# Bringing the top-one results back tile by tile inside the memory stage, splitting the 32-expert weights there, and letting the second product lag by three units

## The chip, the cores and the metric

The kernel runs on one NeuronCore of a Trainium2 chip. The core has five engines with a queue of instructions each: TensorE (PE in the rows; its weight loads are PEld), VectorE (DVE), ScalarE (ACT), GpSimd (POOL) and SyncE (SP, which here only starts transfers). An engine runs its queue in the order in which it was written and waits on semaphores for the others. The metric is the time of one execution on the device in microseconds (us).

## What is computed

The input is 4 sequences of 1024 tokens with 128 channels, in float32. Two layers follow each other, each with a token mixer and an expert network:

```python
x = x + rwkv6_time_mixing(layernorm(x))       # stage 1
x = x + top1_of_8_experts(layernorm(x))       # stage 2, 128 -> 512 -> 128, relu
x = x + quaternion_memory(layernorm(x))       # stage 3, first part
x = x + top4_of_32_experts(layernorm(x))      # stage 3, second part, 128 -> 64 -> 128, swiglu
```

The memory takes keys and values (`x @ Wk.T + bk`, `x @ Wv.T + bv`) as quaternions, makes the keys unit length, sums value times key along the sequence, multiplies the running sum with the conjugate key, divides by the root of the position, normalizes, and projects with `Wo`. The last network takes softmax scores over 32 experts, keeps the four best of each token (with a capacity for each expert), computes `(silu(x @ W1) * (x @ W3)) @ W2` for them and adds one shared expert for all.

## The kernel before

The 4096 tokens are 32 groups of 128, held in `x_tok` (channels along the free axis); four groups are a tile of 512 tokens, so there are 8 tiles (`TILES`). `build` runs three functions one after the other. Each opens its own block, and between two blocks all engines meet.

**Stage 2, `top1_experts` (L622).** Tokens are sorted by expert into rows of DRAM. The loop `over_rows` runs 39 tiles of 128 rows, and GpSimd writes each result back to the DRAM tensor `results` with an indirect transfer (L1092). At its end stand three more pieces of work. The weights of the 32 experts, three tensors of 128 x 2176 (`d_raw`), are split in a rounded high part (`make_hi`, ScalarE, L1174) and the rest (`make_lo`, L1181, one on VectorE and two on GpSimd), since TensorE multiplies them in rounded float32 as three products. SyncE waits for all result rows and brings them back in four transfers (L788). VectorE adds them to `x_tok` in four pieces (L1028). Then the block ends.

**Stage 3, `memory_and_top4` (L1193).** Its planner `weave` (L1357) writes each engine's queue from small functions that name a step. VectorE first sets constants (L1814 to L1823). `norm(i)` normalizes tile i (statistics L1600, step 4), `ahead(i)` makes keys and values, `main(i)` forms value times key (`c_bound`, L1641 on VectorE, L1967 on GpSimd), sums along the sequence on TensorE (L1472) and multiplies with the key again (`c_read`, L1658, L1973), `tail(i)` normalizes and projects (`c_got` L1672, `c_shift` L1687, `x_tok` L1692). After a prologue with `norm(0)`, `ahead(0)`, `norm(1)` come 8 bodies. In body i stand, step by step of 16, `tail(i-1)`, `main(i)`, `ahead(i+1)`, `norm(i+2)`.

Then come 8 tiles of 17 expert units (one shared, 16 pairs). In unit n TensorE makes h1 into `bank_1` and h3 into `bank_3` (three products each, L1507 to L1509), then the second product of unit n-2 (`second`, L1555 to L1558). ScalarE applies silu (L1920), VectorE multiplies with h3 (L1789) and with the routing weights `w_wide` (`hidden`, L1798), ScalarE rounds the result (`hid_hi`, L1930) and GpSimd takes the rest (`hid_lo`, L2000), which the third part of `second` needs. `silu`, `hidden`, `hid_hi` and `hid_lo` have two buffers each. h3 of unit n may overwrite its bank once `hidden` of n-2 is done. Between the units stand the routing of the next tile (`route`, at units 0 to 16, most of its small VectorE work after units 5 to 8 and 11), the statistics of the tile after (`look`; its `look_shift` L1711 after unit 6) and the end of the tile before (`end`: copy of the sum at unit 3, transposes L1589 at unit 4, the add of `x_tok` L1811 at unit 5). SyncE loads `w_wide` for a tile from DRAM in eight transfers of 512 KB.

## Time and profile before

| | us |
|---|---|
| three timed runs | 896.37, 898.77, 899.38 |
| median | 898.77 |
| the profiled execution | 899.56 |
| span of its trace | 897.7 |
| stage 2 ends with its last `x_tok` add, the next block's first VectorE instruction starts | 403.90, 406.88 |
| the expert units start | 551.0 |

| engine | busy us | share |
|---|---|---|
| TensorE | 765.0 | 85% |
| VectorE | 633.8 | 71% |
| GpSimd | 485.7 | 54% |
| ScalarE | 464.0 | 52% |

The profile gives for each instruction its start, duration and inputs, and for the idle time ahead of it which instruction of another engine ended it. Shares of busy time are averages over stages with different limits, so they are read stage by stage. Durations of matmuls overlap, since they are pipelined: two of one kind that follow each other start 0.23 us apart though each shows 0.40.

### The profile page before, as it was taken

How to read it: one execution, taken by the hardware profiler on the slowest of the kernel's cores; microseconds unless marked ns; L12 is line 12 of the kernel's file. 1: busy time of each engine (PE TensorE's matmuls, PEld its weight loads, DVE VectorE, ACT ScalarE, POOL GpSimd, SP SyncE). 2: the span in 40 equal slices, each digit the busy share in tenths (PEclk: the TensorE clock that was granted, in tenths of full speed). 3: DMA queues.
4: the chain of work that ended last, by engine and by line, in shares of the span. 5: the costliest groups of instructions: out<-in, count | busy, mean ns of one | idle time of the engine just before them, and what ended most of it. 6: DMA issues, size and time to landing. Idle time of an engine off the chain costs nothing.

```text
span 897.7 us, 14530 instructions
## 1 busy us (share of the span) xinstructions
PE 765.0 (85%) x3937; PEld 567.5 (63%) x3938; DVE 633.8 (71%) x1453; ACT 464.0 (52%) x918; POOL 485.7 (54%) x440
## 2 busy tenths in 40 slices
PE   5999999996486499912889998999999999999997
PEld 2444444542386499912778786677768686868685
DVE  3789999986564255574587876768686868786764
ACT  3455555652121377722464645656656565756453
POOL 2677777773046344561355653555555555555554
PEclk9999999997555699965899999899999999999998
DMA  5000000000491122220000003545547281909180
GB/s 178 0 1 1 1 0 0 0 1 0 93 375 47 42 66 68 62 106 1 1 2 1 1 1 81 112 91 112 115 88 142 61 168 36 191 20 195 38 166 12
DMA packets 35663, 60.08 MB, mean 67 GB/s; under 512 B 3488, under 2 KB 15264, under 8 KB 34960
## 3 DMA queue, kind: packets, MB, share of 16 engines
q1 hardware_dynamic: 33328, 54.67, 26.1%
q0 software_dynamic: 2272, 4.67, 1.5%
q8 instruction: 27, 0.44, 0.2%
q14 instruction: 36, 0.29, 0.1%
HBM read 51.04 MB, written 8.28 MB: 66 GB/s over the span
## 4 chain that ended last, share of the span: by engine, by line
PE 26%; issue 12%; POOL 11%; DVE 3%; ACT 2%; POOLq 0%; ACTq 0%; DVEq 0%
POOL d_hid_lo L2000 6%; PE c_m L1507 2%; PE c_m L1509 2%; PE c_m L1508 2%; PE c_o L1558 1%; PE c_r L1558 1%; PE c_k L1507 1%; POOL c_bound L1967 1%; PE c_r L1488 1%; PE c_k L1508 1%; PE c_k L1509 1%; POOL c_read L1973 1%; PE c_o L1556 1%; PE c_o L1555 1%; PE c_v L1509 1%
## 5 line engine op out<-in xcount | busy, mean ns | idle before, releaser
L2000 POOL TENSOR_TENSOR d_hid_lo<-c_bound,d_hid_hi 128x512 fp32r<-128x512 f32 x136 | 176.4, 1297 | 157.5 <-ACT d_hid_hi L1930 155.5
L1930 ACT ACTIVATE d_hid_hi<-c_bound 128x512 fp32r<-128x512 f32 x136 | 85.2, 626 | 45.3 <-DVE c_bound L1798 44.9
L576 POOL TENSOR_TENSOR a_rs<-a_r,a_state 128x512 f32<-128x512 f32 x64 | 75.2, 1186 | 29.9 <-DVE a_state L419 28.0
L419 DVE TENSOR_TENSOR_SCAN a_state<-a_decay,a_state,a_vb 128x512 f32<-128x512 f32 x64 | 81.1, 1269 | 0.0
L1092 POOL DMA_INDIRECT results<-b_y_row,b_result_row x39 | 37.4, 960 | 51.1 <-DVE b_y_row L1008 29.8
L1789 DVE TENSOR_TENSOR c_m<-c_bound,c_m 128x512 f32<-128x512 f32 x64 | 44.2, 691 | 26.8 <-PE c_m L1509 20.9
L1789 DVE TENSOR_TENSOR c_v<-c_bound,c_v 128x512 f32<-128x512 f32 x64 | 44.2, 691 | 24.3 <-PE c_v L1509 19.0
L1507 PE MATMUL c_m<-d_x_hi,d_hi 128*128 128x512 f32 x136 | 56.1, 413 | 1.8 <-DVE c_bound L1798 1.6
L999 DVE TENSOR_TENSOR b_hidden<-b_h,b_b 128x512 f32<-128x512 f32 x39 | 27.0, 691 | 42.9 <-PE b_h L835 42.2
L1509 PE MATMUL c_m<-d_x_hi,d_lo 128*128 128x512 f32 x136 | 54.1, 398 | 0.0
L1508 PE MATMUL c_m<-d_x_lo,d_hi 128*128 128x512 f32 x136 | 54.0, 397 | 0.0
L1920 ACT ACTIVATE c_bound<-c_k 128x512 f32<-128x512 f32 x60 | 35.7, 596 | 34.7 <-PE c_k L1509 34.2
L1920 ACT ACTIVATE c_bound<-c_m 128x512 f32<-128x512 f32 x60 | 35.7, 595 | 34.4 <-PE c_m L1509 34.0
L403 DVE TENSOR_TENSOR a_vb<-a_k,a_vb 128x512 f32<-128x512 f32 x64 | 43.1, 685 | 10.4 <-PE a_vb L307 10.4
L559 POOL TENSOR_TENSOR a_xf<-a_lerp,a_xt 128x512 f32<-128x512 f32 x40 | 43.3, 1092 | 10.3 <-DVE a_lerp L396 10.2
L1086 POOL DMA_INDIRECT rows_in<-b_rows,b_index x32 | 31.0, 970 | 31.6 <-DVE b_index L939 22.8
L835 PE MATMUL b_h<-b_xin_t,b_w_now 128*128 128x128 f32 x312 | 43.5, 284 | 0.8 <-ACT b_xin_t L1061 0.4
L843 PE MATMUL b_y<-b_w,b_hidden_t 128*128 x312 | 42.8, 280 | 0.9 <-ACT b_hidden_t L1072 0.7
L1798 DVE TENSOR_TENSOR c_bound<-c_v,d_w_wide 128x512 f32<-128x512 f32 x56 | 38.7, 691 | 6.6 <-DMA d_w_wide<-pair_weights 4.1
L306 PE MATMUL a_vb<-a_v_hi,a_spread 128*128 128x512 f32 x64 | 41.4, 647 | 1.0 <-issue 0.7
L835 PEld LDWEIGHTS b_h<-b_xin_t,b_w_now 128*128 128x128 f32 x312 | 39.6, 199 | 1.9 <-ACT b_xin_t L1069 0.8
L1798 DVE TENSOR_TENSOR c_bound<-c_m,d_w_wide 128x512 f32<-128x512 f32 x56 | 38.7, 691 | 2.5 <-POOL d_hid_lo L2000 0.7
(306 smaller groups left out, 2178.4 us busy)
## 6 DMA issues: line engine op xcount, KB each, us to landing
d_w_wide<-pair_weights SPq DMA_DIRECT2D x64, 512.0 KB, 11.8
b_w<-in_w SPq DMA_DIRECT2D x2, 2048.0 KB
d_raw<-in_moe SPq DMA_DIRECT2D x3, 1088.0 KB
b_xin<-rows_in SPq DMA_DIRECT2D x39, 64.5 KB
b_rows<-results SPq DMA_DIRECT2D x4, 512.0 KB, 5.0
out<-c_read SPq DMA_DIRECT2D x8, 256.0 KB, 2.5
a_weights<-in_mixing SPq DMA_DIRECT2D x1, 901.0 KB
shape_consts<-in_consts SPq DMA_DIRECT2D x1, 744.0 KB
```

The source lines that it names most:

```text
L419: dve.tensor_tensor_scan(state[:, j, seq_cols(h, 1)], decay[:, h, :], vb[j % 3][:, :], first, ALU.mult, ALU.add).then_inc(scan_ready, 1)
L559: pool.tensor_tensor(xf[:, f, :], lerp[:, (f + h) % 2, :], xt[h][:, 1:TILE + 1], ALU.add).then_inc(xf_ready, 1)
L576: pool.tensor_tensor(rs[:, j, :], rr[:, h, :], state[:, j, seq_cols(h, 0)], ALU.mult).then_inc(rs_ready, 1)
L835: mm = pe.matmul(bank_h[h][:, f * P:(f + 1) * P], w1_now[:, h, f * P:(f + 1) * P], xin_t[:, h, :], start=True, stop=True)
L1507: pe.matmul(out, weights_hi, moving_hi, start=start, stop=False)
L1508: pe.matmul(out, weights_hi, moving_lo, start=False, stop=False)
L1509: return pe.matmul(out, weights_lo, moving_hi, start=False, stop=stop)
L1789: dve.tensor_tensor(bank_3[r][:, :], silu[:, r, :], bank_3[r][:, :], ALU.mult).then_inc(product_ready, 1)
L1798: dve.tensor_tensor(hidden[:, r, :], bank_3[r][:, :], w_wide[:, u - 1, :], ALU.mult).then_inc(hidden_ready, 1)
L1920: act.activation(silu[:, r, :], bank_1[r][:, :], ACT.Silu).then_inc(silu_ready, 1)
L1930: act.activation(hid_hi[:, r, :], hidden[:, r, :], ACT.Copy).then_inc(hi_ready, 1)
L2000: pool.tensor_tensor(hid_lo[:, r, :], hidden[:, r, :], hid_hi[:, r, :].bitcast(F32), ALU.subtract).then_inc(lo_ready, 1)
```

## The change

**The split.** The raw weights no longer have tensors of their own: they are loaded into the first 13 of the 16 slices of `w_wide`, which is idle until the expert units. `split_operands` is gone. ScalarE makes the high parts in twelve pieces of 128 x 544, two in each of bodies 0 to 5 (steps 13 and 15). VectorE makes all the rests in twelve such pieces, two in each of bodies 1 to 6 (steps 11 and 15), and some small casts in body 1.

**The results.** SyncE waits for the result rows at the start of stage 3 and brings back one tile at a time into the last three slices of `w_wide` (`BACK_RING` = 3), a further one when a slice has been used. VectorE adds it in step 3 of `norm`, ahead of the statistics. Tiles 0 and 1 are added in the prologue, tiles 2 to 7 in bodies 0 to 5. `results` and `row_stored` are now made in `build`.

**The units.** `second` lags three units (`LAG`) where it lagged two; `hid_hi` and `hid_lo` have three buffers (`HALVES`), `hidden` still two. The steps of `end` move back by one unit each. The constants of stage 1 are freed after it; the unit matrix is kept as `ident`.

```diff
+LAG = 3
+RAW_PAIRS = -(-3 * UNITS * P // TILE)
+BACK_RING = PAIRS - RAW_PAIRS
+SPLITS = 4
+HALVES = 3
...
@@ top1_experts
-                for n in range(4):
-                    sp.wait_ge(row_stored[n], 16 * len(range(n, ROW_TILES, 4)))
-                by_token = results[0:TOKENS, :].rearrange("(p g) c -> p g c", p=P)
-                for n in range(4):
-                    part = slice(n * GROUPS // 4, (n + 1) * GROUPS // 4)
-                    sp.dma_start(back[:, part, :], by_token[:, part, :]).then_inc(come_back[n], 16)
-
+                sp.wait_ge(moe_loaded, 16 * len(moe_in))
...
-                make_small(dve)
-                make_lo(dve, 0)
-                for n in range(4):
-                    dve.wait_ge(come_back[n], 16)
-                    part = slice(n * GROUPS // 4, (n + 1) * GROUPS // 4)
-                    dve.tensor_tensor(x_tok[:, part, :], x_tok[:, part, :], back[:, part, :], ALU.add)
...
-                make_hi(act)
...
-                make_lo(pool, 1)
-                make_lo(pool, 2)
...
@@ memory_and_top4, SyncE
+                def bring_back(i):
+                    sp.dma_start(returned(moe, i), by_token[:, SUB * i:SUB * i + SUB, :]).then_inc(come_back[i % BACK_RING], 16)
+
                 def norm(i, h, step):
+                    if step == 5 and i + BACK_RING < TILES:
+                        sp.wait_ge(x_back, i + 1)
+                        bring_back(i + BACK_RING)
...
+                for n in range(4):
+                    sp.wait_ge(row_stored[n], 16 * len(range(n, ROW_TILES, 4)))
+                for i in range(BACK_RING):
+                    bring_back(i)
...
@@ TensorE
-                    if u >= 2:
-                        second(i, h, u - 2)
-                    elif not (isinstance(i, int) and i == 0):
-                        second(i - 1, 1 - h, UNITS - 2 + u)
+                    if u >= LAG:
+                        second(i, h, u - LAG)
+                    elif i > 0:
+                        second(i - 1, 1 - h, UNITS - LAG + u)
...
@@ VectorE
+                    if step == 3:
+                        dve.wait_ge(come_back[i % BACK_RING], 16 * (i // BACK_RING + 1))
+                        x = x_tok[:, SUB * i:SUB * i + SUB, :]
+                        dve.tensor_tensor(x, x, returned(moe, i), ALU.add).then_inc(x_back, 1)
...
+                    if step in (11, 15) and 0 < i <= 3 * SPLITS // 2:
+                        make_lo(2 * i - 2 if step == 11 else 2 * i - 1)
+                    if step == 14 and i == 1:
+                        dve.tensor_copy(strict[:, :], dw("strict"))
+                        dve.tensor_copy(ones_b[:, :], dw("ones"))
+                        dve.wait_ge(wg_made, 1)
+                        dve.tensor_tensor(wg_lo[:, :], dw("wg"), wg_hi[:, :].bitcast(F32), ALU.subtract).then_inc(small_made, 1)
...
                 def end(i, h, u):
-                    if u == 5:
+                    if u == 6:
...
@@ ScalarE
+                    if step in (13, 15) and i < 3 * SPLITS // 2:
+                        c = 2 * i if step == 13 else 2 * i + 1
+                        n, cols = split_cols(c)
+                        act.activation(hi[n][:, cols], raw_operand(moe, n)[:, cols], ACT.Copy).then_inc(hi_made, 1)
...
@@ split
-                    need(act, unit_out, n - 1)
-                    act.activation(hid_hi[:, r, :], hidden[:, r, :], ACT.Copy).then_inc(hi_ready, 1)
+                    need(act, unit_out, n + 1 - HALVES)
+                    act.activation(hid_hi[:, n % HALVES, :], hidden[:, r, :], ACT.Copy).then_inc(hi_ready, 1)
```

How the queues differ is shown at three places of VectorE's. The names are tiles: `d_` those of the 32-expert network, `c_` those of the memory.

At the changeover, VectorE's queue of before (the branch to L1594 is where the engines meet):

```order
L1008 TENSOR_TENSOR b_y_row<-b_y,b_b 128x128
L1185 CAST d_strict<-d_small 128x128
L1186 CAST d_ones<-d_small 128x128
L1188 TENSOR_TENSOR d_wg_lo<-d_small,d_wg_hi 128x32
L1181 TENSOR_TENSOR d_lo<-d_raw,d_hi 128x2176
L1028 TENSOR_TENSOR x_tok<-x_tok,b_rows 128x1024 x4
L749 UNCONDITIONAL_BRANCH
L1594 UNCONDITIONAL_BRANCH
```

And of the changed kernel, on to the first statistics:

```order
L999 TENSOR_TENSOR b_y_row<-b_y,b_b 128x128
L745 UNCONDITIONAL_BRANCH
L1587 UNCONDITIONAL_BRANCH
...
L1831 CAST c_bias<-memory_weights 64x1536
L1834 TENSOR_TENSOR c_bias<-memory_weights,c_bias 1x1536
L1593 TENSOR_TENSOR x_tok<-x_tok,d_w_wide 128x512
L1598 BN_STATS c_stats<-x_tok 128x6 x4
```

Eight instructions left the end of stage 2, and one add of 128 x 512 stands ahead of the first statistics.

In a memory body, VectorE's queue of before, from the second reading of the keys to the statistics:

```order
L1658 TENSOR_TENSOR c_read<-c_key,c_v 128x512 x2
L1664 TENSOR_TENSOR c_real<-c_v,c_key 128x256
L1664 TENSOR_TENSOR c_real<-c_memory_n,c_key 128x256
L1692 TENSOR_TENSOR x_tok<-c_o,c_kept 128x512
L1672 SCALAR_TENSOR_TENSOR c_got<-c_real,c_r 128x512
L1641 TENSOR_TENSOR c_bound<-c_key,c_v 128x512 x2
```

And of the changed kernel, some rows further on as well:

```order
L1669 TENSOR_TENSOR c_read<-c_key,c_v 128x512 x2
L1636 TENSOR_TENSOR d_lo<-d_w_wide,d_hi 128x544
L1675 TENSOR_TENSOR c_real<-c_v,c_key 128x256
L1675 TENSOR_TENSOR c_real<-c_memory_n,c_key 128x256
L1703 TENSOR_TENSOR x_tok<-c_o,c_kept 128x512
L1636 TENSOR_TENSOR d_lo<-d_w_wide,d_hi 128x544
L1683 SCALAR_TENSOR_TENSOR c_got<-c_real,c_r 128x512
...
L1617 TENSOR_REDUCE c_norm<-c_square 128x128
L1593 TENSOR_TENSOR x_tok<-x_tok,d_w_wide 128x512
L1698 SCALAR_TENSOR_TENSOR c_shift<-c_moments,c_rstd 128x4
L1598 BN_STATS c_stats<-x_tok 128x6 x4
```

Two pieces of the split stand between `c_read` and `c_got`, and the add of the results ahead of `c_shift`.

Between expert units 5 and 7, VectorE's queue of before:

```order
L1795 SCALAR_TENSOR_TENSOR c_bound<-c_v,d_w_wide 128x512
L1811 TENSOR_TENSOR c_read<-x_tok,c_x 128x512
L1735 TENSOR_REDUCE d_total<-d_exps 128x4
L1737 RECIPROCAL d_inverse<-d_total 128x4
L1789 TENSOR_TENSOR c_m<-c_bound,c_m 128x512
L1798 TENSOR_TENSOR c_bound<-c_m,d_w_wide 128x512
L1740 TENSOR_TENSOR d_scores<-d_exps,d_inverse 128x128
L1744 MAX d_top<-d_scores 128x8 x4
L1711 SCALAR_TENSOR_TENSOR d_shift<-d_moments,d_rstd 128x4
```

And of the changed kernel:

```order
L1806 SCALAR_TENSOR_TENSOR c_bound<-c_v,d_w_wide 128x512
L1746 TENSOR_REDUCE d_total<-d_exps 128x4
L1748 RECIPROCAL d_inverse<-d_total 128x4
L1800 TENSOR_TENSOR c_m<-c_bound,c_m 128x512
L1809 TENSOR_TENSOR c_bound<-c_m,d_w_wide 128x512
L1822 TENSOR_TENSOR c_read<-x_tok,c_x 128x512
L1751 TENSOR_TENSOR d_scores<-d_exps,d_inverse 128x128
L1755 MAX d_top<-d_scores 128x8 x4
L1722 SCALAR_TENSOR_TENSOR d_shift<-d_moments,d_rstd 128x4
```

The add of the output (`c_read<-x_tok,c_x`) moved from ahead of unit 6 to behind it, so that it is now followed by the scores and `d_shift`.

## Rows read from the trace of the kernel before

**Rows 1.** Busy time by stretch: from:to, us, then per engine, clock, DMA.
```profile
461.00:476.00 15.00, 13.70 (x106) 12.00 (x104) 11.74 (x34) 8.51 (x23) 8.84 (x9) 1.00 0.01 2
...
655.00:697.00 42.00, 40.26 (x192) 30.77 (x191) 32.14 (x68) 25.98 (x48) 23.13 (x20) 1.00 0.53 109
```

**Rows 2.** Timeline of the changeover: start, us, engine, line, [idle before <- releaser].
```profile
386.19 0.96 POOL L1092 DMA_INDIRECT results<-b_y_row,b_result_row  x1 [0.94 <-DVE b_y_row L1008]
...
388.57 1.76 SPq L788 DMA_DIRECT2D b_rows<-results  x4
...
392.38 2.41 DVE L1181 TENSOR_TENSOR d_lo<-d_raw,d_hi 128x2176 fp32r<-128x2176 f32 x1
...
394.72 9.18 DVE L1028 TENSOR_TENSOR x_tok<-x_tok,b_rows 128x1024 f32<-128x1024 f32 x4
...
406.88 0.06 DVE L1814 MEMSET c_eps<- 128x4 f32 x1 [2.98 <-PEq L2020]
...
410.63 0.87 DVE L1600 BATCH_NORM_STATS2 c_stats<-x_tok 128x6 f32<-128x128 f32 x4
```

**Rows 3.** Instructions on the tile b_rows: landing time of its four returning transfers.
```profile
DMA to landing us min/median/max: 3.7/5.0/6.2
```

**Rows 4.** Timeline of one memory body, VectorE, GpSimd and ScalarE.
```profile
470.36 1.28 DVE L1658 TENSOR_TENSOR c_read<-c_key,c_v 128x512 f32<-128x512 f32 x2
...
470.41 2.52 POOL L1973 TENSOR_TENSOR c_read<-c_key,c_memory_n 128x512 f32<-128x512 f32 x2 [1.12 <-DVE c_memory_n L1652]
...
471.90 1.30 DVE L1664 TENSOR_TENSOR c_real<-c_memory_n,c_key 128x256 f32<-128x256 f32 x1
...
472.88 2.69 POOL L1967 TENSOR_TENSOR c_bound<-c_key,c_value_n 128x512 f32<-128x512 f32 x2
...
475.68 0.69 DVE L1672 SCALAR_TENSOR_TENSOR c_got<-c_real,c_r 128x512 f32<-128x512 f32 x1 [1.87 <-issue]
...
477.13 0.60 ACT L1848 ACTIVATE c_key<-c_k 128x512 f32<-128x512 f32 x1 [3.59 <-PE c_k L1449]
...
480.27 1.22 DVE L1687 SCALAR_TENSOR_TENSOR c_shift<-c_moments,c_rstd 128x4 f32<-128x4 f32 x1 [0.83 <-POOL c_rstd L1983]
```

**Rows 5.** Timeline of the last memory body, one GpSimd and one VectorE instruction.
```profile
541.33 1.02 POOL L1994 TENSOR_TENSOR d_rstd<-d_var_eps,c_minus_half 128x4 f32<-128x4 f32 x1
...
541.79 0.29 DVE L1740 TENSOR_TENSOR d_scores<-d_exps,d_inverse 128x128 f32<-128x128 f32 x1
```

**Rows 6.** Timeline of the expert units, TensorE at its last waits.
```profile
562.19 0.80 PE L1558 MATMUL c_r<-d_hid_lo,d_hi 128*128 128x512 f32 x1 [0.60 <-POOL d_hid_lo L2000]
...
671.05 0.40 PE L1556 MATMUL c_r<-d_hid_hi,d_lo 128*128 128x512 f32 x1
...
672.04 0.50 PE L1558 MATMUL c_r<-d_hid_lo,d_hi 128*128 128x512 f32 x1 [0.58 <-POOL d_hid_lo L2000]
```

**Rows 7.** Timeline of the expert units, VectorE and GpSimd.
```profile
576.05 1.28 POOL L2000 TENSOR_TENSOR d_hid_lo<-c_bound,d_hid_hi 128x512 fp32r<-128x512 f32 x1 [0.49 <-ACT d_hid_hi L1930]
...
576.25 1.10 DVE L1711 SCALAR_TENSOR_TENSOR d_shift<-d_moments,d_rstd 128x4 f32<-128x4 f32 x1
...
656.17 0.69 DVE L1786 SCALAR_TENSOR_TENSOR c_bound<-c_bound,c_m 128x512 f32<-128x512 f32 x1 [0.38 <-PE c_v L1509]
...
661.37 1.31 POOL L2000 TENSOR_TENSOR d_hid_lo<-c_bound,d_hid_hi 128x512 fp32r<-128x512 f32 x1 [0.97 <-ACT d_hid_hi L1930]
...
669.27 0.69 DVE L1798 TENSOR_TENSOR c_bound<-c_v,d_w_wide 128x512 f32<-128x512 f32 x1
```

**Rows 8.** Busy time by stretch where the granted clock rises.
```profile
434.00:435.00 1.00, 1.00 (x7) 1.00 (x7) 1.00 (x5) 0.86 (x4) 0.00 (x0) 0.50 0.00 0
...
435.00:436.00 1.00, 1.00 (x7) 0.79 (x6) 0.81 (x7) 0.33 (x2) 0.19 (x1) 0.90 0.00 0
```

**Rows 9.** Timeline, TensorE: the same product at either clock.
```profile
420.81 2.07 PE L1449 MATMUL c_v<-memory_weights,c_xt 128*128 128x128 f32 x8
...
436.17 1.16 PE L1449 MATMUL c_v<-memory_weights,c_xt 128*128 128x128 f32 x8
```

More of the change, by code:

```diff
@@ L695, in top1_experts @@
         hidden_t = sb("hidden_t", [P, 2, D_FF])
-        back = rows[:, :, :].rearrange("p g c -> p (g c)")[:, 0:TOKENS].rearrange("p (g c) -> p g c", g=GROUPS)
         bank_x = [bank(f"x{n}") for n in range(2)]
@@ L714, in top1_experts @@
         row_loaded = [sem(f"row_loaded{n}") for n in range(4)]
-        row_stored = [sem(f"row_stored{n}") for n in range(4)]
         row_t_out, row_t_ready, h_out, h_ready = sem("row_t_out"), sem("row_t_ready"), sem("h_out"), sem("h_ready")
@@ L718, in top1_experts @@
         ht_ready, y_out, y_ready = sem("ht_ready"), sem("y_out"), sem("y_ready")
-        come_back = [sem(f"come_back{n}") for n in range(4)]
         CHOICE = 5
@@ L763, in _ @@
                     sp.dma_start(tensor[:, :], source).then_inc(early_loaded, 16)
-                load_moe(sp)
+                for tensor, source in zip((moe["small"][:, :], *(raw_operand(moe, n) for n in range(3))), moe_in):
+                    sp.dma_start(tensor, source).then_inc(moe_loaded, 16)
                 sp.wait_ge(early_loaded, 16 * len(early))
@@ L1248, in memory_and_top4 @@
         early_n = late_value
+        come_back = [sem(f"come_back{n}") for n in range(BACK_RING)]
+        x_back = sem("x_back")
+        hi_made, lo_made, wg_made, small_made = sem("hi_made"), sem("lo_made"), sem("wg_made"), sem("small_made")
         half_set, rounded, bias_ready = sem("half_set"), sem("rounded"), sem("bias_ready")
@@ L1355, in memory_and_top4, with split_cols @@
         BY_TANH = (4, 5)
+        def split_cols(c):
+            n, part = divmod(c, SPLITS)
+            width = UNITS * P // SPLITS
+            return n, slice(part * width, (part + 1) * width)
         def weave(engine, norm, ahead, main, tail, look, route, unit, end):
@@ L1400, in _, with ahead @@
             def _(sp):
+                by_token = results[0:TOKENS, :].rearrange("(p g) c -> p g c", p=P)
+                def bring_back(i):
+                    sp.dma_start(returned(moe, i), by_token[:, SUB * i:SUB * i + SUB, :]).then_inc(come_back[i % BACK_RING], 16)
                 def norm(i, h, step):
+                    if step == 5 and i + BACK_RING < TILES:
+                        sp.wait_ge(x_back, i + 1)
+                        bring_back(i + BACK_RING)
+                def ahead(i, h, step):
                     pass
-                ahead = main = tail = look = unit = norm
+                main = tail = look = unit = ahead
                 def route(i, h, u):
@@ L1422, in end @@
                 def end(i, h, u):
-                    if u == 6:
+                    if u == 7:
                         sp.wait_ge(out_ready, i + 1)
@@ L1998, in unit @@
                     pool.wait_ge(hi_ready, n + 1)
-                    need(pool, unit_out, n - 1)
-                    pool.tensor_tensor(hid_lo[:, r, :], hidden[:, r, :], hid_hi[:, r, :].bitcast(F32), ALU.subtract).then_inc(lo_ready, 1)
+                    need(pool, unit_out, n + 1 - HALVES)
+                    pool.tensor_tensor(hid_lo[:, n % HALVES, :], hidden[:, r, :], hid_hi[:, n % HALVES, :].bitcast(F32),
+                                       ALU.subtract).then_inc(lo_ready, 1)
                 def end(i, h, u):
```

86 lines of the change are left out of this document (41 added, 45 removed).

## The prediction

> **What bounds the kernel now.** I read the page's busy shares first, then the busy time by stretch, then the timeline where engines wait. The kernel has three stages, and the change touches three places with three different limits.
>
> The expert units are close to TensorE's limit: it is busy 40.26 us of 42 [rows 1]. What it still waits for is short and repeats in each tile: the third part of a second product waits for `hid_lo` from GpSimd (0.58 us in the row) [rows 6].
>
> A memory body takes 15.0 to 15.3 us. No engine fills it: TensorE 13.70, VectorE 11.74, GpSimd 8.84 of 15 [rows 1]. It is a ring: VectorE works from `c_got` to `c_read` almost without a break, and TensorE's sums then lead to the next `c_got`. VectorE's spare time in it stands in two rows: 1.87 us ahead of `c_got` and 0.83 us ahead of `c_shift` [rows 4]. Work that fits there is free, other VectorE work lengthens the body.
>
> The changeover is pure loss for TensorE. GpSimd has issued its last result row at 386.19 + 0.96 = 387.15. VectorE's share of the split and the `x_tok` adds end at 394.72 + 9.18 = 403.90, the engines meet, VectorE starts the next block at 406.88 after 2.98 us of idle time, and takes the first statistics at 410.63 [rows 2].
>
> **The changeover, part by part.** All of the work between 387.15 and 403.90 leaves the end of stage 2. If the meeting still costs 2.98 us (the same engines, the same clearing of semaphores), VectorE starts at 387.15 + 2.98 = 390.13. Its constants take what they took, 410.63 - 406.88 = 3.75 us, so it is ready for tile 0 at 393.88. SyncE starts the transfers at about 390.13; it need not wait for result rows, because before it could start at 388.57 what waits for the same semaphores [rows 2]. The nearest price of the fetch is the landing time of the four old transfers, 3.7 to 6.2 us for 512 KB each [rows 3]; the new ones have 256 KB, so I take the low end. They land at 393.8, just hidden under the constants. If they take 6.2, 2.5 us of the gain are lost. The add of tile 0 is half of an old piece; the old one shows a quarter of 9.18 us with GpSimd in the way, so the nearest undisturbed instruction is `x_tok` L1692's kind at 0.69 us for 128 x 512, `c_got` in rows 4. First statistics at about 394.57 instead of 410.63: **-16.1 us**.
>
> **What comes back in the memory stage.** The add of tile 1 stands in the prologue, behind a reduction which the chain to the next `c_xn` passes through: +0.7. That of tile 2 lies in body 0, where TensorE runs at half clock and VectorE waits for it: 0. Those of tiles 3 to 7 stand in bodies 1 to 5, right where VectorE waits 0.83 us for `c_rstd` (0.69 fits in 0.83) [rows 4]: 0, if GpSimd's small `c_rstd` instruction doesn't hold VectorE up. It didn't in one place: `d_scores`, with both inputs in SBUF, took its 0.29 us while `d_rstd` ran from 541.33 to 542.35 [rows 5].
>
> The Trainium skill, page "SBUF — State Buffer", section "Who interferes with whom", says otherwise: a VectorE instruction with two SBUF inputs is fully blocked by a GpSimd instruction that reads SBUF and came first, until that ends. By it each of the five adds would be a wait plus 0.69 us late. Rows 5 don't agree for this small instruction, rows 4 do for large ones.
>
> For the large ones the trace is plain: `c_real` with both inputs in SBUF takes 1.30 us where its own work is about 0.4, since it waits until GpSimd's second `c_read` has ended at 470.41 + 2.52 = 472.93; it then goes first, and GpSimd's next instruction is the one that waits [rows 4]. A piece of the split (128 x 544, both inputs in SBUF) costs a quarter of 2.41 us [rows 2], 0.60. The first piece asks at about 471.56, when `c_read` on VectorE ends, 0.1 us ahead of the border between GpSimd's two instructions (470.41 + 1.26 = 471.67). If it wins that border, it runs to 472.3, GpSimd's second `c_read` ends at 473.5, `c_real` at 473.8, `x_tok` at 474.4, the second piece waits for the next border at 475.0 and ends at 475.6, just ahead of `c_got` at 475.68. Cost 0. If it misses it, everything is one GpSimd instruction later and `c_got` comes at 476.9: +1.2 for each of six bodies. I take the first with a small allowance: +0.5 in all. GpSimd's `c_bound` then ends up to 1.2 us later, which its reader on TensorE has in hand. The casts and `d_wg_lo` in body 1 each ask for the port too; one GpSimd instruction more, +1.0. The pieces on ScalarE (nearest row 0.60 for 128 x 512) are two per body and lie in its 3.59 us wait [rows 4]: 0. Sum of the memory stage: **+2.2 us**, between +0.7 and +12.
>
> **The units.** With three units' lag, `hid_lo` is ready one unit earlier than it is needed. The wait at 672.04 goes: the part before started at 671.05 and parts follow each other every 0.23 us, so 672.04 - 671.05 - 0.23 = 0.76 us, 0.8 with the slow restart [rows 6]. Is another wait late next? TensorE is held by VectorE until `hidden` of unit 9 is done at 669.27 + 0.69 = 669.96, because h3 of unit 11 needs its bank. That wait stays. Behind it TensorE has second(8), the ranks, h1 of unit 12 and then h3 of unit 12, which needs `hidden` of unit 10, done some 1.3 us after that of unit 9. So nothing replaces the removed wait. -0.8 in each of tiles 0 to 6, where a routing makes VectorE late; tile 0 has one more at its start (562.19) [rows 6]: -0.8.
>
> Then the moved `end`. Its transposes leave the front of unit 5, so h3 of unit 5 comes sooner and VectorE's 0.38 us wait there shrinks to about 0.1 [rows 7]: -0.3. But the output's add now stands ahead of the scores, which pushes `d_shift` (two SBUF inputs) from 661.37, where it went just ahead of GpSimd's `hid_lo` starting at 661.37, into that instruction. What that costs shows in tile 0, which has no such add ahead of it: GpSimd from 576.05, `d_shift` from 576.25 for 1.10 us instead of 0.14 [rows 7]. `hidden` of unit 9 comes later by this; less the 0.3 and the slack ahead of unit 6's silu, about +0.5 for each of tiles 1 to 5 (tile 6 has no `look`). So tile 0: -1.6; tiles 1 to 5: -0.8 + 0.5 = -0.3 each, -1.5; tile 6: -1.1. Sum **-4.2 us**, between -9 (no block, -1.2 per tile) and +1 (block, and the wait comes back in another place). At the end of the kernel three second products are left instead of two, but they lie beside the last unit's product, rounding and rest: 0.
>
> **Sum.** 899.56 - 16.1 + 2.2 - 4.2 = 881.5 for the profiled execution. The median of the three runs stands 0.8 lower (898.77), so I forecast 880.7, rounded 881.
>
> **The rivals.**
> - *Units gain in full* (`d_shift` gets through): five times 0.9 more, about 4.5, 876.5. For: its delay depends on 0.2 us. Chance 0.15.
> - *The units gain nothing*: the wait for `hid_lo` turns into one for `hidden`, since `hidden` still has two buffers. 881 + 4.2 = 885. Against: the count above. 0.15.
> - *The memory bodies pay*: each piece misses its border (6 x 1.2) and each of five adds is late by 0.7. 7.2 - 0.5 + 3.5 = 10.2 more, 891. By the section of the Trainium skill named above the adds' 3.5 alone would come, 884.5. 0.14.
> - *The changeover gives less*: the meeting, the fetch or the first add costs 2.5 to 4 us more, 884. 0.10.
> - *Slower than before: the clock.* TensorE's granted clock is 0.50 (1.2 GHz) up to 435 and rises after continuous work from 430 on [rows 8]. A group of eight matmuls takes 2.07 us there against 1.16 at 2.4 GHz [rows 9]. If VectorE's extra waits keep TensorE from rising, a body of 13.70 us busy becomes 13.70 x 1.78 = 24.4, +9.4. It decides from the third such body on: 881 + 28 = 909. Against: the adds and pieces leave TensorE's gaps about as long as they are. 0.03.
> - *The change doesn't do what it says*: the next block's start doesn't move, because something else holds the meeting. Nothing in rows 2 between 387.15 and 403.90 is left that could. 0.01, 897.
>
> My forecast's case has 0.42. The range from 872 to 890 holds it, the first two rivals, the fourth, and half of the third. Faster by over 0.3% (2.7 us, what a measurement of this kernel can tell from no change): 0.95; within: 0.02; slower: 0.03.
>
> **What would show it.** In the changed trace: first `c_stats` 7.5 us after the last indirect store is issued, with no wait for a transfer ahead of the first add. Bodies 1 to 5 of 15.0 to 15.6 us, adds of 0.69 and not 1.3, `c_got` still with an idle time ahead of it. In the units no wait of TensorE for `hid_lo`, periods shorter by some 0.3 to 0.5 us, and `d_shift` at 1.1 instead of 0.14. It is wrong if bodies grow by over 1 us or if TensorE's waits for `hidden` grow by what those for `hid_lo` lose.

## Result and the profile after

The changed kernel takes **885.84 us** (median of 4 runs, 883.27 to 886.19) against 899.08 us of the kernel before beside it: ratio 0.985, 95% interval 0.982 to 0.988. The forecast was 881, between 872 and 890. The profiled execution spans 884.3 us instead of 897.7.

To see where the 13.4 us went I cut both executions at four instructions: the start of the last indirect store, the first statistics of stage 3 (`c_stats`), and the first and the last `hid_lo` on GpSimd.

| stretch | before | after | change | forecast |
|---|---|---|---|---|
| start to last indirect store | 386.19 | 387.36 | +1.2 | 0 |
| to the first statistics | 24.44 | 12.65 | -11.8 | -16.1 |
| to the first `hid_lo` (memory stage) | 144.41 | 146.45 | +2.0 | +2.2 |
| to the last `hid_lo` (units) | 334.78 | 330.21 | -4.6 | -4.2 |
| to the end | 7.9 | 7.6 | -0.3 | 0 |

The first two rows hold the whole miss. The +1.2 is not the change's by all that shows: in the twelve kernels of this document, whose first two stages have nearly the same work up to there, the last store starts anywhere from 381.4 to 387.4 (385.7 to 387.4 in all but two), and the kernel before lies among the others with its 386.19. The -11.8 is the change's.

The changeover after, where [rows 2] showed it before (timeline; start, us, engine, line, and in brackets the idle time before and its releaser):

```profile
387.36 0.96 POOL L1076 DMA_INDIRECT results<-b_y_row,b_result_row  x1 [0.94 <-DVE b_y_row L999]
395.53 0.06 DVE L1825 MEMSET c_eps<- 128x4 f32 x1 [8.96 <-PEq L2041]
...
395.58 4.75 SPq L1375 DMA_DIRECT2D d_w_wide<-results  x4
...
397.50 1.75 DVE L1834 TENSOR_TENSOR c_bias<-memory_weights,c_bias 1x1536 fp32r<-1x1536 f32 x1
399.28 0.69 DVE L1593 TENSOR_TENSOR x_tok<-x_tok,d_w_wide 128x512 f32<-128x512 f32 x1
400.01 0.87 DVE L1598 BATCH_NORM_STATS2 c_stats<-x_tok 128x6 f32<-128x128 f32 x4
```

The constants take 3.75 us as before, the add of tile 0 takes 0.69 and has no wait for a transfer ahead of it: all as forecast. But GpSimd has issued its last store at 388.32, no engine has work, and VectorE starts at 395.53, **7.21 us** later instead of 2.98.

What happens in them stands in another view, the instructions of one source line, here the line that opens stage 2's block (columns: queue, kind, duration in ns min/median/max, start). After:

```profile
L745 DVEq DRAIN  x1: 303/303/303, 386.3 to 386.3; - x1
L745 POOLq DRAIN  x1: 7067/7067/7067, 387.1 to 387.1; - x1
```

and the same line of the kernel before:

```profile
L749 POOLq DRAIN  x1: 15792/15792/15792, 389.5 to 389.5; - x1
...
L749 DVEq DRAIN  x1: 7803/7803/7803, 396.1 to 396.1; - x1
```

At the end of a block each engine executes a DRAIN, which holds until its earlier work is done. VectorE's ends with its last instruction. GpSimd's doesn't. After, it ends at 387.1 + 7.07 = 394.2, 5.9 us behind the last store's instruction. Before, it ended at 389.5 + 15.79 = 405.3, which is again 5.9 us behind GpSimd's last instruction, the piece of the split that ended at 387.64 + 11.78 = 399.42. So before the change the 5.9 us ran beside VectorE's `x_tok` adds (to 403.90), and of the 2.98 us that I read as the price of the meeting, the first 1.4 (403.90 to 405.3) were the end of this drain. After, the 7.21 us are 5.9 of drain and 1.3 from its end to VectorE's start.

A memory body after, where [rows 4] showed one before:

```profile
455.69 1.01 POOL L2000 TENSOR_TENSOR c_rstd<-c_var_eps,c_minus_half 128x4 f32<-128x4 f32 x1
455.82 0.68 DVE L1593 TENSOR_TENSOR x_tok<-x_tok,d_w_wide 128x512 f32<-128x512 f32 x1
...
456.73 1.23 DVE L1698 SCALAR_TENSOR_TENSOR c_shift<-c_moments,c_rstd 128x4 f32<-128x4 f32 x1 [0.23 <-POOL c_rstd L2000]
...
461.80 3.01 POOL L1990 TENSOR_TENSOR c_read<-c_key,c_memory_n 128x512 f32<-128x512 f32 x2 [1.12 <-DVE c_memory_n L1663]
462.96 0.72 DVE L1636 TENSOR_TENSOR d_lo<-d_w_wide,d_hi 128x544 fp32r<-128x544 f32 x1
...
465.62 1.20 DVE L1636 TENSOR_TENSOR d_lo<-d_w_wide,d_hi 128x544 fp32r<-128x544 f32 x1
467.08 0.69 DVE L1683 SCALAR_TENSOR_TENSOR c_got<-c_real,c_r 128x512 f32<-128x512 f32 x1 [0.27 <-issue]
```

The add takes 0.68 us although GpSimd's `c_rstd` was first, and lies in the wait ahead of `c_shift`, which shrank from 0.83 to 0.23. The first piece of the split got between GpSimd's two `c_read` (they take 3.01 together instead of 2.52), and the idle time ahead of `c_got` fell from 1.87 to 0.27: used up, but not overrun.

The units after, where [rows 6] and [rows 7] showed them before (VectorE, GpSimd, TensorE):

```profile
650.24 1.30 POOL L2017 TENSOR_TENSOR d_hid_lo<-c_bound,d_hid_hi 128x512 fp32r<-128x512 f32 x1 [0.46 <-ACT d_hid_hi L1947]
...
650.61 0.96 DVE L1722 SCALAR_TENSOR_TENSOR d_shift<-d_moments,d_rstd 128x4 f32<-128x4 f32 x1
...
656.43 0.50 PE L1496 MATMUL c_m<-d_x_hi,d_hi 128*128 128x512 f32 x1 [1.13 <-DVE c_bound L1809]
...
660.09 0.50 PE L1496 MATMUL c_v<-d_x_hi,d_hi 128*128 128x512 f32 x1 [1.29 <-DVE c_bound L1809]
```

No wait for `hid_lo` is left but one of 0.6 us at the very end of the kernel, and `d_shift` (128 x 4) takes 0.96 us, because it asks 0.4 us after GpSimd's `hid_lo` has started. Counted from the tile's first `hid_lo`, `d_shift` comes at 14.7 us instead of 14.9, not later than before; it is GpSimd's instruction that moved further, from 14.9 to 14.3, since unit 6's products no longer stand behind the output's add.

### The profile page after: what moved, and what is told of

It reads as the page before. It is cut to its first block, busy times and chain, and to the rows that moved or that the text cites. A ratio compares the mean times of both kernels' runs of the same rounds, so it can differ in the third digit from the quotient of the medians.

```text
span 884.3 us, 14563 instructions
## 1 busy us (share of the span) xinstructions
PE 759.0 (86%) x3937; PEld 572.3 (65%) x3938; DVE 639.8 (72%) x1468; ACT 463.6 (52%) x927; POOL 479.7 (54%) x438
## 4 chain that ended last, share of the span: by engine, by line
PE 31%; issue 8%; POOL 7%; DVE 6%; ACT 2%; DMA 1%; POOLq 0%; SPq 0%; DVEq 0%; ACTq 0%
PE c_m L1496 3%; PE c_m L1498 3%; PE c_m L1497 3%; POOL d_hid_lo L2017 2%; PE c_v L1496 1%; PE c_k L1496 1%; PE c_o L1550 1%; PE c_k L1497 1%; PE c_k L1498 1%; POOL c_bound L1984 1%; PE c_o L1547 1%; PE c_o L1548 1%; POOL c_read L1990 1%; PE c_v L1498 1%; PE c_r L1550 1%
## 5 line engine op out<-in xcount | busy, mean ns | idle before, releaser
L1076 POOL DMA_INDIRECT results<-b_y_row,b_result_row x39 | 37.5, 960 | 51.9 <-DVE b_y_row L999 35.3
L834 PEld LDWEIGHTS b_y<-b_w,b_hidden_t 128*128 128x128 f32 x312 | 38.5, 194 | 3.0 <-issue 2.1
```

The costliest lines, as they stand in the source:

```text
L834: mm = pe.matmul(bank_y[h][:, 0:P], hidden_t[:, h, f * P:(f + 1) * P], w2[:, bass.ds(e * D_FF + f * P, P)], start=(f == 0), stop=(f == FF_ ...
```

## Experiments

Every kernel is compared with the kernel before, run beside it on the same chip. "Changed" is the changed kernel. It did not run beside the others, so a difference to it carries about 1 us of doubt (the kernel before has medians of 899.08 to 900.08, and 895.30 in a single run); where a difference is smaller than some 2 us, only the stretches of the traces tell it.

| kernel | us | before beside it | ratio, 95% interval |
|---|---|---|---|
| changed | 885.84 | 899.08 | 0.985 (0.982 to 0.988) |
| c_gp_filler | 890.23 | 900.08 | 0.990 (0.987 to 0.994) |
| c_no_drain | 880.13 | 900.08 | 0.978 (0.975 to 0.982) |
| c_mid_drain | 884.95 | 900.08 | 0.984 (0.980 to 0.988) |
| c_skip_first | 880.50 (one run) | 899.32 | |
| b_skip | 894.01 (one run) | 895.30 | |
| u_lag_two | 890.86 | 900.08 | 0.990 (0.986 to 0.994) |
| u_shift_first | 880.92 | 899.32 | 0.980 (0.977 to 0.984) |
| u_end_early | 878.83 (one run) | 895.30 | |
| m_small_early | 884.77 (one run) | 899.32 | |
| best1 | 875.63 | 899.32 | 0.975 (0.972 to 0.978) |

### Is it the drain? Work put ahead of it, the drain left out

> The changed kernel with one more GpSimd instruction at the end of stage 2, a subtraction of 128 x 2176 behind the last indirect store (some 5.8 us by the 11.78 us that two of them took in rows 2); its result is not used, nothing is left out. In the changed kernel GpSimd's drain at the end of the block starts at 387.1 and ends at 394.2, 5.9 us after the last indirect store's instruction (387.36 + 0.96 = 388.32); in the kernel before it ended at 405.3, 5.9 us after the last piece of the split (387.64 + 11.78 = 399.42). Theory: a drain on GpSimd, after it has issued indirect transfers, costs 5.9 us counted from the end of its last instruction, however long ago the transfers landed. So the meeting moves by the whole filler: kernel 5.5 to 6.0 us slower than the changed one (885.8), about 891.5. Rival, the drain only waits until the last store's data has landed: the filler lies in that wait, 0 to 0.5 us, about 886. Rival, the meeting costs 7 us after the last engine for another reason (code of the next block): also 5.5 to 6 slower, but then the runs without the drain show no gain.

```diff
                 over_rows(pool, tile)
+                more = rows[:, 0:17, 0:P]
+                pool.tensor_tensor(more, more, more, ALU.subtract)
```

The timeline, and the drain by its source line:

```profile
386.04 0.96 POOL L1076 DMA_INDIRECT results<-b_y_row,b_result_row  x1 [0.94 <-DVE b_y_row L999]
387.03 3.82 POOL L1081 TENSOR_TENSOR b_rows<-b_rows 128x2176 f32<-128x2176 f32 x1
398.06 0.06 DVE L1827 MEMSET c_eps<- 128x4 f32 x1 [12.81 <-PEq L2043]
...
L745 POOLq DRAIN  x1: 10879/10879/10879, 385.9 to 385.9; - x1
```

The filler took 3.8 us instead of 5.8 (why is open; the two of rows 2 shared their time with VectorE's work). The drain ends at 396.8, again 5.9 us behind GpSimd's last instruction (390.85 = 387.03 + 3.82), and VectorE starts 12.02 us after the last store's start instead of 8.17: 3.85 us later, the whole filler. The kernel is 4.4 us slower than the changed one. A drain that only waited for the data to land would have hidden it, so that rival falls.

> The changed kernel with stage 2 ended without GpSimd's drain, and with the two later drains of GpSimd and the clearing of semaphores between stages 2 and 3 left out too (stage 3 takes other semaphores; all that the results need is waited for by SyncE as before). Theory (the 5.9 us are GpSimd's drain): VectorE starts stage 3 about 1 us after the last indirect store's instruction instead of 7.2 us, SyncE's fetch then waits 1 us for the last store to land; first statistics 5 to 6 us earlier; kernel 5 to 6 us faster than the changed one, about 880. Rival (landing of stores or code of the next block holds the start): 0 to 1 us faster, about 885.

```diff
-        with nc.Block() as block:
+        with nc.Block(no_gpsimd_drain=True) as block:
...
         with nc.cleanup_on_exit():
             top1_experts(...)
-        with nc.cleanup_on_exit():
             memory_and_top4(...)
```

```profile
386.15 0.96 POOL L1076 DMA_INDIRECT results<-b_y_row,b_result_row  x1 [0.94 <-POOLq L745]
386.21 0.06 DVE L1825 MEMSET c_eps<- 128x4 f32 x1 [0.85 <-PEq L745]
...
388.53 4.14 SPq L1375 DMA_DIRECT2D d_w_wide<-results  x4
391.63 0.69 DVE L1593 TENSOR_TENSOR x_tok<-x_tok,d_w_wide 128x512 f32<-128x512 f32 x1 [1.71 <-DMA d_w_wide<-results]
```

VectorE now makes its constants while the last store is still being issued, SyncE's fetch waits until 388.53 for it to land, and the add waits 1.71 us for the fetch. First statistics stand 6.2 us behind the last store's start instead of 12.65. 5.7 us faster than the changed kernel, as the theory had it. What is late next is the fetch, which the drain had covered.

But the drain's time came back in another place. At the end of stage 3 stands another such drain, here by its source line, first in this kernel, then in the next but one (c_skip_first), which keeps the clearing between the stages:

```profile
L1369 POOLq DRAIN  x1: 7214/7214/7214, 870.1 to 870.1; - x1
```
```profile
L1369 POOLq DRAIN  x1: 1377/1377/1377, 871.1 to 871.1; - x1
```

GpSimd's last instruction ends at 871.38 and 872.38. In c_skip_first the drain ends 0.06 us behind it; here it ends at 877.3, again 5.9 us behind, though the last indirect transfer lies 480 us back. From the last `hid_lo` to the end this kernel takes 8.73 us where the changed one takes 7.59: 0.8 for the drain, which otherwise hides under other engines' last work, and 0.3 behind it, mostly a longer clearing (0.76 us instead of 0.52).

### What sets the 5.9 us?

> The changed kernel with one more drain of GpSimd, right behind the 32 indirect stores of the routing, where GpSimd then waits 12 to 13 us for the first result row. Theory A, the drain's time is a fixed cost: it adds 5.9 us there, hidden, and the drain at the end still takes 5.9 us behind the last instruction; time unchanged, about 886. Theory B, the drain's time grows with the indirect transfers issued since the last drain (71 of them for 5.9 us, 0.083 each): the one at the end falls to 39 x 0.083 = 3.2 us and the kernel gets 2.6 us faster, about 883. Theory C, the drain waits for landing: unchanged, and the extra drain is short or ends with the landing of the last of the 32.

```diff
                         pool.indirect_dma_start(rows_in, ..., rows[:, g, :], None).then_inc(scattered, 16)
+                pool.drain()
```

The last scatter on the timeline, then the new drain and the one at the end, by source line:

```profile
297.39 0.96 POOL L1070 DMA_INDIRECT rows_in<-b_rows,b_index  x1 [0.30 <-issue]
...
L1072 POOLq DRAIN  x1: 12632/12632/12632, 288.4 to 288.4; - x1
...
L745 POOLq DRAIN  x1: 4430/4430/4430, 385.7 to 385.7; - x1
```

The drain behind the 32 scatters ends at 301.0, 2.7 us behind the last one's instruction (298.35). The one at the end, with 39 stores behind the first drain, ends at 390.1, 3.2 us behind its last (386.92). And 71 gave 5.9. Three points on one line, 0.082 to 0.084 us for each indirect transfer since the last drain: theory B. First statistics come 10.0 us behind the store's start, 2.6 sooner. The median is only 0.9 better than that of the changed kernel. The trace shows what can hide the 2.6, for the profiled execution alone: in the last memory body it had a mean clock of 0.66 over 5 us where the changed kernel's had 1.00 (busy time by stretch; the column after the engines is the clock; first this kernel, then the changed one, both 25 us behind the `c_got` of body 5), and its tile 0 of the units took 48.65 us instead of 47.75.

```profile
532.20:537.20 5.00, 4.49 (x37) 4.41 (x36) 4.60 (x11) 0.00 (x0) 2.51 (x2) 0.66 0.00 0
```
```profile
536.90:541.90 5.00, 4.49 (x51) 4.28 (x50) 4.54 (x11) 0.95 (x3) 2.51 (x2) 1.00 0.00 0
```

> The changed kernel without GpSimd's drain at the end of stage 2's block, but with the drains and the clearing of semaphores that follow it. Theory (what costs is the first plain drain of GpSimd behind indirect transfers, wherever it stands): the 5.9 us move to the plain drain behind the clearing, VectorE's start of stage 3 stays about 7 us after the last store's instruction, time unchanged, about 885. Rival (only the block's own drain is dear): VectorE starts 1.5 to 2 us after the store, about 880, as in the run without any of them.

Only the first of the two edits of c_no_drain. The line is now that of the scope around the block (two drains, the clearing between them):

```profile
L2041 POOLq DRAIN  x2: 58/596/1133, 385.9 to 387.4; - x2
...
L2041 POOLq EVENT_SEMAPHORE_RANGE_CLEAR  x1: 269/269/269, 387.1 to 387.1; - x1
```

Here my theory fell and the rival held. The first drain, the one ahead of the clearing, ends at 387.05, 0.1 us behind the last store's instruction, though 71 indirect transfers stand before it; the plain one behind the clearing takes 0.06 us. First statistics 6.3 us behind the store's start, 880.5 us, like the kernel without any of them, and the last drain of the kernel costs nothing either (above). So not every drain behind indirect transfers costs 5.9 us: the one ahead of the clearing doesn't, and behind it and the clearing no later one does. Which of the two, that drain or the clearing, takes the cost away is not shown. One argument of the block takes the 5.9 us away, and unlike c_no_drain it gives none of them back at the end.

### How much of the 2.98 was the meeting?

> The kernel before the change, with stage 2's block ended without GpSimd's drain; nothing else. In the kernel before, VectorE's last x_tok add ends at 403.90, GpSimd's drain at 405.3, and VectorE starts stage 3 at 406.88, 2.98 us after its last add. Theory (of the 2.98 us only 1.1 to 1.6 are the engines' meeting, the rest is the end of GpSimd's drain, and the forecast carried the 2.98 over as if it were the meeting): VectorE starts 1.1 to 1.6 us after its last add, first statistics 1.4 to 1.9 us sooner, kernel about 1.5 us faster than before (897.5 against 899.1). Rival (the meeting costs 2.98 us by itself, and the drain is another cost that only shows in the changed kernel): the gap stays at 2.9 to 3.0 us.

The diff is the same one line, in the kernel before.

```profile
394.55 4.62 DVE L1028 TENSOR_TENSOR x_tok<-x_tok,b_rows 128x1024 f32<-128x1024 f32 x4
```
```profile
  DVE c_eps L1814: 1.5, 1
```

(The second is from the view of the scope's line: who waited for it, us, times.) The adds took 4.62 us instead of 9.18, because this time GpSimd's two pieces of the split went first and VectorE's `d_lo` was the one that waited (7.03 us instead of 2.41); the last add ends 17.8 us behind the last store's start here and 17.7 in the kernel before, so that this changes nothing. VectorE starts 1.5 us behind its last add, and the first statistics come 23.0 us behind the last store's start instead of 24.4. So the meeting itself is 1.5 us here (in the changed kernel 1.3 behind the drain's end, 0.8 behind the last store's in c_skip_first), and 1.4 to 1.5 of the 2.98 belonged to the drain. That settles the failed step from the side of the kernel before. The times of the two single runs, 1.3 us apart, would not tell it.

### The units

> The changed kernel with the units' part undone: a lag of two units, two buffers for hid_hi and hid_lo, and the steps of the output one unit earlier, as in the kernel before. Theory (units give 4.6 us between the first and the last hid_lo, and 0.3 behind it; the memory stage and the changeover are untouched by it): 4.5 to 5.0 us slower than the changed one, about 890.7, TensorE's waits for hid_lo back in each tile, period of a tile 42.08 instead of 41.69. Rival, the gain in the units came from another part (other addresses of buffers, the clock, the order of the loads): 0 to 2 us slower, 886 to 888.

```diff
-LAG = 3
+LAG = 2
-HALVES = 3
+HALVES = 2
```

and the output's four steps at units 3, 4, 5, 6 again. 5.0 us slower than the changed kernel, as expected; by the ratios to the kernel before beside each it is 4.0 (9.2 and 13.2 us faster than it). The profiled execution shows more, 6.2 us in the units, and 3.1 of them are tile 0 (50.87 us against 47.75), where the clock stood at 0.50 for 10.2 us here and for 6.8 there. So the totals are the weaker evidence. From the first `hid_lo` of a tile to that of the next, tiles 1 to 5 take 42.08 or 42.09 us, as in the kernel before (42.07 to 42.09); 41.68 or 41.69 in the changed one. The waits of TensorE from 560 us on, that is behind the start of tile 0, first u_lag_two, then the changed kernel (sum of us, times, longest):

```profile
PE c_r L1550 <- POOL d_hid_lo L2017: 4.8, 9, 0.6
PE c_o L1550 <- POOL d_hid_lo L2017: 3.6, 6, 0.6
PE c_v L1496 <- DVE c_bound L1809: 1.7, 6, 0.4
PE c_m L1496 <- DVE c_bound L1809: 1.6, 5, 0.4
```
```profile
PE c_m L1496 <- DVE c_bound L1809: 7.5, 7, 1.3
PE c_v L1496 <- DVE c_bound L1809: 7.3, 6, 1.3
```

> The changed kernel with d_shift of tiles 3 to 7 moved in VectorE's order of unit 6: right behind the output's add, ahead of the scores and the four MAX instructions, instead of behind them. In the changed kernel it asks at 650.6, while GpSimd's hid_lo runs from 650.24 to 651.54, and takes 0.96 us instead of 0.14; behind it the whole routing of VectorE is late, and TensorE waits 1.13 and 1.29 us for hidden in the two units after it. Theory of the forecast (the blocked d_shift costs the units most of what the lag of three could give): d_shift 0.14 us again, it ends ahead of hid_lo's start, the period of a tile falls from 41.69 by 0.5 to 0.9 in the five tiles with such a step, kernel 2.5 to 4.5 us faster than the changed one, about 882. Rival (TensorE's waits for hidden come from the routing's own length on VectorE, and another instruction, d_scores or MAX, is blocked in place of d_shift): period 41.5 to 41.7, 0 to 1 us faster, about 885.5.

```diff
                 def look(i, h, u):
...
-                    if u == 6:
+                    if u == 6 and i < 3:
+                        shift_of(i)
...
                 def end(i, h, u):
                     if u == 6:
...
                                           ALU.add).then_inc(out_ready, 1)
+                        if i + 3 < TILES:
+                            shift_of(i + 3)
```

(`shift_of` holds the old instruction.)

```profile
647.16 0.68 DVE L1826 TENSOR_TENSOR c_read<-x_tok,c_x 128x512 f32<-128x512 f32 x1
647.75 0.16 DVE L1726 SCALAR_TENSOR_TENSOR d_shift<-d_moments,d_rstd 128x4 f32<-128x4 f32 x1
```

0.16 us instead of 0.96, and the tiles take 40.86 to 40.90 us instead of 41.69: 0.82 each, the whole block of `d_shift`, 4.1 us in five tiles. The kernel is 4.9 us faster than the changed one. Nothing else was blocked in its place.

> The changed kernel with the lag of three units, but the four steps of the output (copy of y, its transposes, the add, the store) in the units where they stood before (3, 4, 5, 6 instead of 4, 5, 6, 7). The add is then again ahead of unit 6's product, and nothing stands between the product and the scores. Theory (the add's new place pushed d_shift into hid_lo; the old place leaves it free): d_shift 0.14 us, period of a tile below 41.69, and above the 40.87 of the kernel with d_shift moved, since the transposes stand ahead of h3 again (0.3 us by rows 7): 41.1 to 41.3. Rival (with the lag of three, y is copied one unit later, and at the old place TensorE's transposes wait for it): period 41.6 to 42.3, with TensorE waiting for c_read in front of L1582.

The output's steps at units 3 to 6 with the lag of three kept. Tiles 1 to 5 take 41.08 to 41.10 us, and the instructions on d_shift's line (ns min/median/max) show it free; the changed kernel's row is below it:

```profile
L1722 DVE SCALAR_TENSOR_TENSOR d_shift<-d_moments,d_rstd x8: 143/143/1089, 513.0 to 769.0; 128x4 f32<-128x4 f32 x8
```
```profile
L1722 DVE SCALAR_TENSOR_TENSOR d_shift<-d_moments,d_rstd x8: 142/958/1103, 519.0 to 775.6; 128x4 f32<-128x4 f32 x8
```

So the lag alone gives 42.08 - 41.10 = 1.0 us a tile. Moving the output's steps, as the change does, takes 0.6 of it back; the block of `d_shift` costs 0.8, and 0.2 (41.10 - 40.87) is what unblocking h3 of unit 5 gives. The traces of tile 2 show it: with the steps at the old place VectorE still waits 0.39 us ahead of the first multiplication of unit 5, in u_shift_first it doesn't wait there, and at the first multiplication behind the scores it is 0.2 us ahead.

### The memory stage

> The changed kernel with the two casts and d_wg_lo on VectorE and d_wg_hi on ScalarE taken out of bodies 0 and 1 of the memory stage and put at the end of stage 2, where GpSimd's drain hides them. Theory (these three instructions are what makes body 1 16.06 us long instead of 14.92, the pieces of the split and the adds are not): body 1 at 14.9 to 15.1, the other bodies as they are, first hid_lo 1.0 us nearer to the first statistics (146.45 us in the changed kernel). Rival (the first pieces of the split on VectorE, or on ScalarE in body 0, cause it): body 1 stays above 15.7.

The two casts, `d_wg_lo` and ScalarE's `d_wg_hi` stand behind `over_rows` in stage 2. From one `c_got` to the next, body 1 takes 14.94 us; in the changed kernel 16.06; bodies 2 to 5 take 14.92 to 14.94 in both. So they are what makes body 1 long, 1.1 us. The distance to the first `hid_lo` fell by 0.5 only (146.0): up to the `c_got` of body 5 this kernel is 1.3 us nearer to the first statistics (0.2 of it already at the `c_got` of body 0), and it loses 0.8 of it between the last two `c_got`. There the clock dipped, to a mean of 0.70 in the stretch of 5 us in which the changed kernel had 1.00 (its row stands with c_mid_drain):

```profile
534.80:539.80 5.00, 5.00 (x45) 4.89 (x45) 4.61 (x11) 0.11 (x1) 2.51 (x2) 0.70 0.00 0
```

That last stretch, from the `c_got` of body 5 to the first `hid_lo`, took 34.6 us in the changed kernel and in five of the ten here, 35.3 to 35.4 in two and 36.1 to 36.2 in three, with the same instructions in nearly all of them. So the edit gives its 1.1 us in body 1, and the clock takes or leaves up to 1.6 behind it.

### The best of them together

> The changed kernel with the three edits that the theories favour together: no drain of GpSimd and no clearing between stages 2 and 3, the small casts and d_wg_lo at the end of stage 2, d_shift ahead of the scores. By the theories 5.7 + 1.0 + 2.5 to 4.5 us faster than the changed kernel, so 875 to 877. If d_shift's place gives nothing, 879; if the casts at the end of stage 2 now delay VectorE's constants (no drain hides them), about 0.5 us more, though the wait for the fetched results (1.7 us in the run without drains) should take them.

875.63 us, 10.2 us faster than the changed kernel and 2.5% faster than before. The tiles take 40.86 or 40.87, body 1 14.92, and VectorE's constants start 0.1 us behind the start of the last store. It leaves out the clearing like c_no_drain, and pays for it alike: 8.74 us from the last `hid_lo` to the end, the last drain 5.9 us behind GpSimd's last instruction. With the block's argument alone (c_skip_first: first statistics only 0.06 us later, end 7.59) it should be about 1.1 us faster still; that is an estimate from those two kernels, not a run.

```profile
385.18 0.18 DVE L1018 TENSOR_TENSOR d_wg_lo<-d_small,d_wg_hi 128x32 fp32r<-128x32 f32 x1
385.68 0.96 POOL L1083 DMA_INDIRECT results<-b_y_row,b_result_row  x1 [0.94 <-POOLq L745]
385.81 0.09 DVE L1837 MEMSET d_used<- 128x32 f32 x1
...
391.26 0.69 DVE L1603 TENSOR_TENSOR x_tok<-x_tok,d_w_wide 128x512 f32<-128x512 f32 x1 [1.77 <-DMA d_w_wide<-results]
```

## Why the prediction was right, and where it was not

**Changeover, -16.1 forecast, -11.8 measured.** The failed step is this one: "If the meeting still costs 2.98 us (the same engines, the same clearing of semaphores)". The number came from a row in which VectorE was the last engine with work, and I took the idle time ahead of it for the price of the meeting. Half of it was the rest of another engine's drain, whose 5.9 us had run since 399.42 under the adds; the meeting itself is 1.3 to 1.5. With the adds gone, all 5.9 us stand in the open: 5.9 + 1.3 = 7.2 instead of 2.98, 4.2 us. Both sides are shown: without that drain the gap in the kernel before is 1.5 us (b_skip), and in the changed kernel the whole start moves by 6.4 (c_no_drain, 12.65 to 6.2 behind the store). The rows that would have told me were in the trace of before, a drain of GpSimd that ended 5.9 us behind its last work; I had listed only what the engines compute. The rest of the step held: constants 3.75, fetch hidden, add 0.69. My fourth rival ("the meeting, the fetch or the first add costs 2.5 to 4 us more", 884, chance 0.10) is the case that came, a little beyond its end; it deserved more, since the 2.98 was the least supported term of the largest item.

**Rival "the change doesn't do what it says".** I wrote that nothing between 387.15 and 403.90 was left that could hold the meeting. Something was, for 5.9 us; it held the meeting only in part.

**Memory stage, +2.2 forecast, +2.0 measured.** Tile 1's add: +0.7, as said. Tile 2's add was put at 0, since TensorE runs at half clock there and "VectorE waits for it"; from `c_norm` to `c_got` body 0 got 0.5 longer (12.43 us against 11.94). In m_small_early, without ScalarE's `d_wg_hi` in that body, it is 12.23, so 0.2 of the 0.5 are not the add's; whether the other 0.3 are, no run tells. The adds of tiles 3 to 7 and the pieces cost nothing: bodies 2 to 5 take 14.92 or 14.93 us, as three of four did before (one took 15.27, which no longer occurs: -0.35). I had allowed 0.5 for the pieces. The casts and `d_wg_lo` cost 1.1 in body 1 (forecast 1.0), and m_small_early shows that it is they, though by which wait is open. The first piece won the border as worked out. Wrong sizes of 0.5 here and there cancelled.

The rule of the Trainium skill ("SBUF — State Buffer", "Who interferes with whom") that I weighed would have given 3.5 us for the adds. These runs side with the rows, for this small instruction: five adds of 0.68 or 0.69 us beside `c_rstd`. For large ones they side with the page: `d_shift` behind `hid_lo` took 0.96 instead of 0.14, `c_shift` behind GpSimd's `c_kept` of 128 x 512 1.23.

**Units, -4.2 forecast, -4.6 measured.** By tile: tile 0 -1.55 (forecast -1.6), tiles 1 to 5 -0.40 each (-0.3), tile 6 -1.05 (-1.1). The mechanism is the one described: the waits for `hid_lo` went, `d_shift` fell into `hid_lo`, and that took back most of what tiles 1 to 5 gained. Only the wording "pushes `d_shift`" is off: `hid_lo` came 0.6 us sooner, `d_shift` 0.2 sooner. u_shift_first puts its price at 0.82 us a tile where I had 0.8 (+0.5 net of the 0.3 that the move gives back), and u_end_early puts that 0.3 at 0.2. The gain of the lag alone, 0.8 in the forecast, is 1.0. Of the fit in tile 0, part is luck: with the same instructions it took 47.6 to 49.5 us in the kernels here (see below), and 47.75 in the profiled one. The two executions in the table happened to have the clock at 0.50 for 6.8 us each, which makes them comparable.

**The sign I named as a warning was badly chosen.** I wrote that the forecast is wrong "if TensorE's waits for `hidden` grow by what those for hid_lo lose". Against u_lag_two, which has the units of the kernel before, they lost 8.4 us behind the start of tile 0 and the others grew by 11.5, and yet each tile is 0.4 us shorter. The block of `d_shift` is not all of that growth: u_end_early, where it is free in tiles 1 to 5, waits 12.0 us for `hidden` against 3.3 in u_lag_two. My reading, which no run tests by itself, is that with a longer lag TensorE has less left to do when it meets the wait for `hidden`, so that wait gets longer. Only the period of a tile decides.

**Range and chances.** 885.84 lies inside 872 to 890, faster had 0.95. The likeliest time was 4.8 us too low, nearly all of it from one term.

## What to carry to other kernels

When work is taken away from in front of a meeting of the engines, read when each engine's drain ends, not only how long the last engine with work sat idle: that idle time contains the rest of the slowest drain, and it grows by what the drain was hidden under. Where GpSimd has issued indirect transfers, count 0.083 us for each in its plain drain and end the block without it, if the readers wait for the transfers themselves. Keep the clearing of semaphores with its own drain behind the block; where both were left out, the 5.9 us stood in the next plain drain, 480 us later. And when a step is moved on VectorE, look at what GpSimd runs at its new time: an instruction of 128 x 4 with both inputs in SBUF cost 0.8 us a tile in one place and nothing where it ran 0.8 us earlier.

## What the runs showed of the hardware

- GpSimd's plain drain takes 0.082 to 0.084 us for each indirect transfer issued since the last drain, counted from the end of its last instruction: 32, 39 and 71 transfers gave 2.7, 3.2 and 5.9 us. The data had long landed: in the kernel before, SyncE, which waits for it, started at 388.57, and the 5.9 us began at 399.42; in c_no_drain they began at 871.38. With none, at the end of stage 1, it ended 0.07 us behind GpSimd's last instruction. Behind the drain ahead of a clearing, and the clearing, it took 0.06 us (c_skip_first). What the engine does in that time is not shown.
- The periods of tiles 1 to 5 and of bodies 2 to 5 repeat to 0.04 us from run to run, so that a single profile tells 0.1 us there. What varies is where the clock falls. At tile 0 of the units TensorE waits 3.7 us for the routing weights, and the granted clock falls to 0.50 (1.2 GHz), for about 7 us in the changed kernel and about 10 in c_no_drain, with the same instructions (busy time by stretch, the changed kernel first, both 11.5 to 15.5 us behind their first `hid_lo`):

```profile
558.00:562.00 4.00, 4.00 (x16) 3.18 (x15) 2.60 (x4) 2.81 (x9) 1.36 (x2) 0.80 1.07 210
```
```profile
550.00:554.00 4.00, 4.00 (x11) 3.05 (x10) 2.08 (x3) 1.83 (x6) 1.28 (x1) 0.50 1.07 210
```

  Tile 0 took 47.75 and 49.15 us in these two. This alone moves the time of a kernel by 1.4 us, more than some of the effects measured here. Why the clock comes back sooner or later is open.
